# Three of sixteen exponential tiles are added by accumulating DMAs in the cross attentions of a two-layer perceiver kernel

## The reference, cut to what matters

```python
# layer 0 (layer 1 is alike, with its own weights, 1/sqrt(32) and mask == 1 -> -1e9)
q = layernorm_per_head(x @ Wq.T + bq) * scale            # 512 x 16 heads x 32
k = layernorm_per_head(kv[:, :, 0]); v = kv[:, :, 1]     # 8192 x 16 x 32
attn = where(padding_mask, q @ k.T, -inf)
p = softmax(attn, axis=-1)                               # exp(a - max) / sum(exp(a - max))
out = (p @ v) @ Wo.T + bo
```

## Time and profile before

| | |
|---|---|
| median of 3 runs (lowest to highest) | 1708.62 us (1704.49 to 1716.28) |
| profiled execution, span from first to last instruction | 1710.0 us |
| TensorE busy | 1608.9 us, 94% of the span |
| VectorE busy | 1028.7 us, 60% |
| ScalarE busy | 522.1 us, 31% |
| GpSimd busy | 100.3 us, 6% |
| mean granted TensorE clock | 0.974 of full speed |
| second half of the cross attention of layer 0, first exponential to last addition | 284.43 to 448.21 us |
| the same of layer 1 | 1177.12 to 1359.83 us |

### The profile page before, as it was taken

One profiled execution on the slowest core, in us unless ns is written; L12 is line 12 of the kernel. 1 busy time (PEld: TensorE's weight loads), 2 busy tenths in 40 slices (PEclk: granted clock), 3 DMA queues, 4 the chain that ended last, 5 costly groups with the idle time before them and its releaser, 6 DMA issues. The chain is left out here.

```text
span 1710.0 us, 27863 instructions
## 1 busy us (share of the span) xinstructions
PE 1608.9 (94%) x9460; PEld 758.6 (44%) x9471; DVE 1028.7 (60%) x1681; ACT 522.1 (31%) x781; POOL 100.3 (6%) x82
## 2 busy tenths in 40 slices
PE   7999999999899889999999899998999899989997
PEld 3333333222343376666665433332222244467775
DVE  6677777999746551111111599998979945652223
ACT  3434434878413310000000211114658612200000
POOL 0200001000002010000000320000300001010001
PEclk9899998999999989999999999998999999989999
DMA  4442332211067967666661423210412021239996
GB/s 167 149 151 110 143 141 82 64 51 37 0 133 124 197 235 256 235 233 225 235 235 57 152 91 117 74 67 32 158 39 74 0 86 32 100 122 336 325 327 228
DMA packets 73420, 240.28 MB, mean 141 GB/s; under 512 B 7328, under 2 KB 20528, under 8 KB 54032
## 3 DMA queue, kind: packets, MB, share of 16 engines
q1 hardware_dynamic: 64752, 220.42, 39.8%
q10 hardware_dynamic: 6048, 10.69, 1.7%
q0 software_dynamic: 2560, 8.39, 1.5%
HBM read 214.04 MB, written 35.91 MB: 146 GB/s over the span
## 5 line engine op out<-in xcount | busy, mean ns | idle before, releaser
L1564 ACT ACTIVATE BIG<-banks 128x1024 f32<-128x1024 f32 (+5 forms) x320 | 282.1, 934 | 122.5 <-PE banks L1510 121.7
L1086 DVE CUSTOM_DVE_ANT_0 BIG<-banks,MASK,MX 128x512 bf16<-128x512 f32 (+5 forms) x384 | 228.9, 656 | 61.8 <-issue 38.3
L2106 PEld LDWEIGHTS banks<-KF,BIG 128*128 128x128 f32 x1792 | 227.0, 191 | 14.1 <-issue 14.1
L2106 PE MATMUL banks<-KF,BIG 128*128 128x160 f32 (+1 forms) x1792 | 229.2, 289 | 2.6 <-DVE KF L1824 2.0
L2134 PE MATMUL banks<-BIG,PB 128*128 128x512 f32 x448 | 202.9, 600 | 0.0
L695 PE MATMUL banks<-KF,XN 32*128 32x512 f32 (+4 forms) x1280 | 188.8, 609 | 11.4 <-DVE MX L1086 3.8
L1503 PE MATMUL banks<-XN,KF 32*128 32x512 f32 (+4 forms) x1280 | 187.9, 614 | 7.4 <-ACT BIG L1564 5.3
L1615 DVE TENSOR_TENSOR PB<-PB,BIG 128x2048 f32<-128x2048 f32 (+5 forms) x78 | 165.7, 2124 | 22.6 <-ACT BIG L1564 20.2
L1079 DVE TENSOR_REDUCE MXW<-banks 128x2 f32<-128x1024 f32 x128 | 150.3, 1216 | 44.6 <-PE banks L706 43.4
L1470 PE MATMUL banks<-BIG,V 128*32 128x512 f32 (+4 forms) x1280 | 160.4, 570 | 5.0 <-issue 2.6
L2134 PEld LDWEIGHTS banks<-BIG,PB 128*128 128x128 f32 x448 | 81.5, 190 | 113.1 <-issue 112.9
(11 more groups left out here) (296 smaller groups left out, 1468.1 us busy)
## 6 DMA issues: line engine op xcount, KB each, us to landing
BIG<-in_L0f_w SPq DMA_DIRECT2D x64, 1024.0 KB, 4.8
BIG<-in_L1f_w SPq DMA_DIRECT2D x48, 1024.0 KB, 5.7
BIG<-in_mask_q SPq DMA_DIRECT2D x16, 1024.0 KB, 8.0
k_saved<-KF SPq DMA_DIRECT2D x32, 256.0 KB, 2.7
CT<-in_ctx SPq DMA_DIRECT2D x6, 1024.0 KB, 4.8
XNT<-in_ctx SPq DMA_DIRECT2D x6, 1024.0 KB, 6.4
v_saved<-V SPq DMA_DIRECT2D x24, 256.0 KB, 2.4
KF<-k_saved SPq DMA_DIRECT2D x24, 256.0 KB, 3.3
```

The costliest lines, as they stand in the source:

```text
L1086: last = v.tensor_tensor_reduce(m.JUNK[:, 2 * half + e, k0:k1], pair[:, e, k0:k1], bias, 1.0, mx, ALU.add, ALU.max, mx)
L1564: a.activation(m.PE_[:, s % NP, 2 * half:2 * half + 2, q0:q1], m.pair[(2 * s + half) % 3][:, :, q0:q1], ACT.Exp).then_inc(exp_ready, 1)
L2106: last = t.matmul(out, W1[k][:, d, f * P:(f + 1) * P], XE[:, d, :], start=d == 0, stop=d == DC - 1)
```

## The change

In the two cross attentions the tiles of steps 3, 7 and 11 of each block (the last key tile of chunks 0, 1 and 2) are not added by VectorE. GpSimd issues a DMA for each, from the tile's place in `PE_` to `PSUMS[c]`, with `accum_op=ALU.add`. It waits for both exponentials of the tile and for VectorE's addition of the step before. A DMA moves 128x2048 float32, 1 MB. With 4 blocks and 2 cross attentions these are 24 DMAs.

The ring `PE_` gets a fifth place, in a part of `BIG` that was free in this stage. Steps 0, 1 and 2 of each four go in turn through places 0, 1 and 2 as before; every fourth step goes to place 3 or to place 4 in turn, so those two places are used again after 8 steps, the others after 4.

```diff
+    dma_summed = [m.sem(f"{n}_dmasum{c}", dyn) for c in range(DC - 1)]
...
+    by_dma = [KT_ * c + KT_ - 1 for c in range(DC - 1)] if dyn else []
+    NV = NS - len(by_dma)
+    FAR = 2 * NP
...
+    def place(s):
+
+        return NP if dyn and s % FAR == FAR - 1 else s % NP
+
+    def before(s):
+
+        return s - (FAR if dyn and s % NP == NP - 1 else NP)
+
+    def summed(i, s):
+
+        return i * NV + sum(x not in by_dma for x in range(s + 1)) + BS
...
+    def tile_summed(act, i, s):
...
+        last = before(s) % NS
+        back = (before(s) - last) // NS
+        if last not in by_dma:
+            act.wait_ge(sum_taken, summed(i + back, last))
+        elif back == 0:
+            act.wait_ge(dma_summed[last // KT_], i * 16 + 16)
+        else:
+            act.wait_ge(sum_taken, summed(i + back, NS - 1))
...
                     times_values(i, s - 1)
+                if dyn:
+                    with pe.If(i + 1 >= nb):
+                        for sem in dma_summed:
+                            pe.wait_ge(sem, i * 16 + 16)
...
         @staticmethod
         def gpsimd(pool, nb):
+
+            def body(i):
+                for s in by_dma:
+                    c = s // KT_
+                    wait_alone(pool, exp_ready, (i * NS + s) * 2 + 2 + B)
+                    wait_alone(pool, sum_taken, summed(i, s - 1))
+                    nc.gpsimd.dma_start(m.PSUMS[c].rearrange("p g n -> p (g n)"),
+                                        m.PE_[:, place(s)].rearrange("p g n -> p (g n)"), accum_op=ALU.add).then_inc(dma_summed[c], 16)
+
+            if dyn:
+                active_loop(pool, nb, body)
             O.gpsimd(pool)
...
+                    if s not in by_dma:
+                        dve.wait_ge(exp_ready, (i * NS + s) * 2 + 2 + B)
+
+                        dve.wait_ge(sum_taken, summed(i, s - 1))
+                        if s == NS - 1 and dyn:
+
+                            for sem in dma_summed:
+                                dve.wait_ge(sem, i * 16 + 16)
...
-        m.PE_ = big(0, 4).rearrange("p (b g n) -> p b g n", b=NP, g=G)
+        m.PE_ = big(0, NP + 1).rearrange("p (b g n) -> p b g n", b=NP + 1, g=G)
```

More of the change, by code:

```diff
@@ L1385, in weighted_values @@
     slots_cleared, next_loaded = m.sem(L.name + "_slots", L.fixed == 0), m.sem(L.name + "_next")
-    m.fresh = []
     n = L.name + "_pv"
     dyn = L.fixed is None
+    dma_summed = [m.sem(f"{n}_dmasum{c}", dyn) for c in range(DC - 1)]
+    m.fresh = []
     mask_loaded, bias_ready, sum_zeroed = m.sem(n + "_mask", dyn), m.sem(n + "_bias", dyn), m.sem(n + "_zeroed", L.fixed == 1)
@@ L1396, in weighted_values, with tile_multiplied @@
     NROW = 4 if whole else 3
-    B = to_raise(m, dyn, {product_done: NP - 1, sum_taken: NP - 1, added_up: 1})
-    BP, BA = (B + NP - 1, B + 1) if dyn else (0, 0)
+    B = to_raise(m, dyn, {product_done: FAR - 1, sum_taken: NP - 1, added_up: 1})
+    BP, BS, BA = (B + FAR - 1, B + NP - 1, B + 1) if dyn else (0, 0, 0)
     O = project_out(nc, m, L, *((None, next_loaded) if dyn else (next_loaded, None)))
-    def tile_free(i, s):
-        return i * NS + s - NP + 1 + BP if dyn else max(0, s - NP + 1)
+    def place(s):
[4 more added lines that the diff above has]
+        return i * NV + sum(x not in by_dma for x in range(s + 1)) + BS
+    def tile_multiplied(i, s):
+        return i * NS + before(s) + 1 + BP if dyn else max(0, s - NP + 1)
+    def tile_summed(act, i, s):
+        if not dyn:
+            act.wait_ge(sum_taken, max(0, s - NP + 1))
+            return
+        last = before(s) % NS
[6 more added lines that the diff above has]
+            act.wait_ge(sum_taken, summed(i + back, NS - 1))
     class Parts:
@@ L1470, in times_values @@
                     last = t.matmul(m.bank[6 + c % 2][rows(g), q0:q1], m.V[:, kt[k], HD * h:HD * h + HD],
-                                    m.PE_[:, s % NP, g, q0:q1], start=k == 0, stop=k == KT_ - 1,
+                                    m.PE_[:, place(s), g, q0:q1], start=k == 0, stop=k == KT_ - 1,
                                     skip_group_check=not dyn)
@@ L1537, in tensor @@
             over_blocks(pe, L, nb, body)
-            O.tensor(pe, sum_taken, nb * NS + BP, added_up, nb * DC + BA)
+            O.tensor(pe, sum_taken, nb * NV + BS, added_up, nb * DC + BA)
         @staticmethod
         def gpsimd(pool, nb):
+            def body(i):
[7 more added lines that the diff above has]
+                active_loop(pool, nb, body)
             O.gpsimd(pool)
@@ L1558, in exponentials @@
                 q0, q1 = L.queries_of[kt[k]]
-                act.wait_ge(product_done, tile_free(i, s))
-                act.wait_ge(sum_taken, tile_free(i, s))
+                act.wait_ge(product_done, tile_multiplied(i, s))
+                tile_summed(act, i, s)
                 for half in range(2):
                     act.wait_ge(scores_ready, (i * NS + s) * 2 + half + 1 + B)
-                    a.activation(m.PE_[:, s % NP, 2 * half:2 * half + 2, q0:q1], m.pair[(2 * s + half) % 3][:, :, q0:q1],
+                    a.activation(m.PE_[:, place(s), 2 * half:2 * half + 2, q0:q1], m.pair[(2 * s + half) % 3][:, :, q0:q1],
                                  ACT.Exp).then_inc(exp_ready, 1)
@@ L1607, in body @@
                         dve.wait_ge(sum_zeroed, c + 1)
-                    dve.wait_ge(exp_ready, (i * NS + s) * 2 + 2 + B)
-                    dve.wait_ge(sum_taken, i * NS + s + BP)
                     dst = m.PSUMS[c][:, :, q0:q1]
-                    if k == 0 and (q0, q1) == (0, T) and not dyn:
-                        v.tensor_copy(dst, m.PE_[:, s % NP]).then_inc(sum_taken, 1)
-                    else:
-                        v.tensor_tensor(dst, dst, m.PE_[:, s % NP, :, q0:q1], ALU.add).then_inc(sum_taken, 1)
+                    if s not in by_dma:
[4 more added lines that the diff above has]
+                                dve.wait_ge(sem, i * 16 + 16)
+                        if k == 0 and (q0, q1) == (0, T) and not dyn:
+                            v.tensor_copy(dst, m.PE_[:, place(s)]).then_inc(sum_taken, 1)
+                        else:
+                            v.tensor_tensor(dst, dst, m.PE_[:, place(s), :, q0:q1], ALU.add).then_inc(sum_taken, 1)
                     if k == 1 and c:
```

## The result

| | before | after |
|---|---|---|
| median of 10 runs (lowest to highest) | 1709.36 us (1703.18 to 1716.28) | 1716.37 us (1709.76 to 1720.09) |
| ratio, 95% interval | | 1.0040 (1.0020 to 1.0059) |
| profiled execution, span | 1710.0 us | 1714.1 us |
| VectorE busy | 1028.7 us | 974.5 us |
| mean granted TensorE clock | 0.974 | 0.973 |

The changed kernel is 7 us slower. That is within the 1% that was forecast as no change and inside the range, yet the interval leaves out 1, so the 7 us need a cause. The two profiled spans are only 4.1 us apart, mainly because the changed kernel came to its first loop 3.04 us earlier and to the second another 1.84 us earlier, in stages that the change doesn't touch.

A forecast was written before the change was run, and what follows sets the result against it. TensorE and ScalarE in lockstep, 38.88 us a block, were taken as the bound. Terms -0.65 - 0.1 + 0.6 = -0.15 us took the profiled 1710.0 to 1709.9 us; forecast 1709 us, no change, range 1700 to 1725.

The forecast's parts named there:

- VectorE isn't the bound: Cross-attention loops: VectorE's additions cost at most 1.1 us today; the rival that VectorE is the bound (1653 us) got 0.02.
- L = 7.8 us: Time of an accumulating DMA from the third exponential tile's end to landing: 6.8 us plus 1.03 us issue; 4.8 to 18 us.
- a cover of 14.0: At a block's edge, the third DMA's L may reach 14.0 us before TensorE waits; cost at 7.8 us: nothing.
- The DMAs' traffic ... the key loads ... are issued 12 steps (28 us) ahead and land in 3.3 us. Both at nothing: In the loops, delay of key loads by the DMAs' 24 MB, and ScalarE's extra wait instructions, were each put at nothing.
- The condition at the inner edges, 0.6 us: TensorE's new condition at six inner block edges: 0 to 0.2 us each, taken as 0.1, so 0.6 us slower.
- The condition at the ends, 0.2 us each: TensorE's new condition at each loop's end, ahead of the sums of chunk 3: 0.2 us each.
- The earlier sums of chunk 3, -0.65 and -0.1 us: At the loops' ends the sums of chunk 3 start 0.65 us earlier in layer 0 and 0.1 us in layer 1.
- VectorE's last additions beside GpSimd's: At layer 0's loop end, additions 61 to 63 meet GpSimd's additions to X, 3.25 us each; the last ends at 447.4.
- the sum of -0.15 us: Whole kernel: loop-end gains of 0.65 and 0.1 us against 0.6 us for the condition at inner edges.
- The chance for larger small losses (1712 to 1715): Rival: larger contention and branch terms, 3 to 6 us slower; a third of the 0.83 for no change.
- the prediction's own signs: Wrong if ScalarE or TensorE waits for VectorE or a DMA at the edges, or the loops' span changes over 3 us.

The follow-up runs named there:

- Late weights: Changed kernel, but in layer 1 the loads of WK and WQ are issued behind the first block's key loads instead of ahead: ratio 1.0006 to the kernel before.
- the kernel with the other edge, the DMAs and both repairs: Changed kernel plus layer 1's WK/WQ loads behind first keys, TensorE's DMA waits once behind the loop, and step 0's edge wait split by half tile: ratio 1.0001.

## Why the prediction came out as it did

- **VectorE isn't the bound: right.** 54.2 us of work left it, a block stays at 38.88 us, and additions cut to nearly nothing gain 0.9 us in two loops (the forecast said at most 1.1).
- **L = 7.8 us: nearly right.** The profile counts 8.2 us from issue to landing. L was to run from the exponential's end, and the issue comes 1.1 us behind that (430.25 against 429.15), as it also waits for VectorE's addition of the step before, which had no term. So L is about 9.3 us, and 13.3 for the slowest third DMA (12.2 us, issued at 1205.08) against a cover of 14.0. No wait for these DMAs is in the trace after. Of the two parts (a fixed part and twice a plain transfer) the second was too small: with the 1.03 us of issue the rule gives 5.8 us for a plain copy, which needed 5.1, and the accumulation adds 3.1 us, not 2.0. The Trainium skill, page "DMA: Bandwidth & Descriptors", section "Anatomy of one DMA — SWDGE (gpsimd) path", has a fit by which 2 MB read would take 6.8 us, an estimate. The DMAs of the last blocks, with no key loads beside them, land in 6.9 to 7.0 us and agree with it; the median of 8.2 us is 1.4 us above it.
- **"The DMAs' traffic ... the key loads ... are issued 12 steps (28 us) ahead and land in 3.3 us. Both at nothing": this step failed.** It holds in layer 0 and at five of six edges. At the first edge of layer 1 it cost 6.6 us (first to last exponential 181.47 against 174.9). I took the share of the DMA engines from one block of layer 0, 0.23, the landing time from a median over 24 loads, and the lead of 28 us from the count of steps. At this edge the lead was 21 us before (1197.90 to 1218.72), with a landing of 10.6 us, and 16.65 us after, with one of 22.6. In the block of layer 1 where three weights of 1 MB and a mask are loaded, the engines were already at 0.97 and 1.05 from 1195 to 1205 without the change. Late weights removed the wait.
- **The condition at the inner edges, 0.6 us: nothing.** Five of the six edges keep their gap (1.46 us, as in the kernel before), and the sixth is the one of the keys.
- **The condition at the ends, 0.2 us each: mis-sized**, 0.57 and 0.62 us (0.35 for the condition, 0.23 for three waits). It was priced by one branch.
- **The earlier sums of chunk 3, -0.65 and -0.1 us: real, but not seen after.** In the kernel with the other edge, the DMAs and both repairs, where the clock is at full speed, the tails are 7.60 and 7.64 us, 0.84 and 0.21 less than before. After the change they are 1.16 and 1.74 us longer: the gap adds 0.6, the sums at a lower clock 1.4, and the wait for VectorE that is gone takes off 0.85 and 0.26. The granted clock was not in my sum at all, and it is the larger part of the loss at the ends.
- **VectorE's last additions beside GpSimd's: right.** Two took 6.04 us, and the last ended at 443.85, which is 446.9 in the time of before (this loop began 3.04 us earlier); forecast 447.4, and TensorE was later anyway.

So the sum of -0.15 us should have been about +9: 6.6 us at one edge and 2.9 us at the ends, together still below 1%. The chance for larger small losses (1712 to 1715) was where the truth lay, and a little beyond, but with other causes than those it listed. That the forecast of no change held rests on its sound part, that VectorE isn't the bound, and on luck: nothing in the sum kept the wait for the values to 6 us. By the prediction's own signs it was wrong here, since TensorE waited for a DMA at an edge and the loop of layer 1 changed by 8.3 us, more than 3.

How far the lower clock follows from the gap stays open. Over 28 ends of loops in 14 kernels the sixteen sums took over 2.2 us (against 1.92) in 9 of 10 ends with a gap of 2.3 us, 3 of 6 with one of 2.0, and 3 of 12 with one of 1.75. That is a tendency and no proof, since each kernel gives one profiled execution and the same gap came with either clock.

## What to carry to other kernels

Moving work from an engine to the DMA queues isn't free because that engine was off the path: look for the stretch where the queues are already full, not at the mean share or the median landing time, and ask which small load stands behind the large ones and how far ahead of its use it is issued there. When an engine shows 99% busy, ask first who waits for it; here nobody did, and giving it 7 us a block was worth 0.1 us a block. And follow a gap at a block's edge to the buffer that is really held before splitting the wait on it.

## What was unexpected of the hardware

- An accumulating DMA of 1 MB within SBUF kept 16 DMA engines for 5.2 us, a plain copy for 2.8 us with nothing beside it (3.0 beside key loads); landing 8.2 against 5.1 us in the median, 6.9 against 4.5 with nothing beside them. The profile counts the same bytes for both.
- With accumulating DMAs and two 1 MB weight loads in flight the issue of a 256 KB load took SyncE 8.14 and 8.39 us instead of 0.34. The share of the DMA engines doesn't tell when: it was 1.07 in that stretch and 1.08 in the run with late weights, where the issue took 0.34.
- After an idle wait of 5.95 us TensorE's granted clock was 0.50 and eight score products took 2.09 us instead of 1.14; short gaps of 2 us ahead of the sums were followed by it in some ends and not in others (3.00 and 1.92 us behind the same gap of 1.99).
